# Adjacency attention on one core: scores by seven products per pair of query tiles in place of eight, with P's low halves on POOL and the mask bias on ACT

## What is computed

```
h = maximum(layernorm(x), 0)
lQ = masked_x @ Wlq ; lK = h @ Wlk ; lV = h @ Wlv + blv
local_scores = where(adj, lQ @ lK.T / 16, -1e9)        # 4096 x 4096
global_scores = gQ @ gK.T / 16 ; es = masked_x @ Wes    # two side columns
max_score = maximum(max(local_scores), global_scores, es)
le, ge, ee = exp(each - max_score) ; denom = sum(le) + ge + ee
res = le/denom @ lV + ge/denom * gV + ee/denom * (masked_x @ Wev + bev)
out = x + maximum(res, masked_x)
```

## Time and profile before

| | |
|---|---|
| median of 3 runs | 790.59 us (790.18 to 790.66) |
| span of the profiled execution | 787.8 us; the runs' median lies 2.8 us above it |
| PE busy | 760.5 us (97%) |
| DVE / ACT / POOL busy | 613.9 / 386.6 / 222.5 us (78 / 49 / 28%) |
| 16 DMA engines busy, hardware queue | 74.5% |
| granted PE clock, mean | 0.996 |

### The profile page before, as it was taken

How to read it: one execution, slowest core, us unless ns; L and a number is a source line. 1 busy time by engine, 2 the same in 40 slices (tenths; PEclk the granted TensorE clock), 3 DMA queues, 4 the chain that set the end, 5 groups by cost and what they waited for, 6 DMA issues and landing times.

```text
span 787.8 us, 15535 instructions
## 1 busy us (share of the span) xinstructions
PE 760.5 (97%) x4200; PEld 424.8 (54%) x4200; DVE 613.9 (78%) x1811; ACT 386.6 (49%) x871; POOL 222.5 (28%) x175
## 2 busy tenths in 40 slices
PE   4799999999999999999999999999999999999995
PEld 3476555555555555555555555555555555555553
DVE  5967677788777778887777788877777888777775
ACT  5757553345555444455554434555544445555442
POOL 2642222332222323322223233223232332132200
PEclk9999999999999999999999999999999999999999
DMA  9983787967778778767677786766777876778656
GB/s 268 227 155 83 145 156 145 174 140 146 144 149 160 148 152 169 147 143 148 141 164 146 154 166 140 156 137 146 162 146 158 167 148 143 143 143 168 119 119 125
DMA packets 334786, 119.92 MB, mean 152 GB/s; under 512 B 303920, under 2 KB 330672, under 8 KB 334768
## 3 DMA queue, kind: packets, MB, share of 16 engines
q1 hardware_dynamic: 334768, 119.70, 74.5%
HBM read 39.98 MB, written 4.19 MB: 56 GB/s over the span
## 4 chain that ended last, share of the span: by engine, by line
PE 82%; issue 7%; DVE 5%; DMA 4%; SPq 1%; ACT 1%; POOL 0%; DVEq 0%; POOLq 0%
PE ps_scores L555 37%; PE ps_u L573 24%; PE ps_u L575 12%; PE ps_q L531 3%; PE ps_v L589 3%; DMA shared<-shared 3%; PE ps_v L602 3%; DMA shared<-x 1%; DVE st L713 1%; DVE shared L805 1%; DVE s L780 1%; DVE w_sq L888 0%; ACT shared L437 0%; DVE q_hl L752 0%; SPq L266 0%
## 5 line engine op out<-in xcount | busy, mean ns | idle before, releaser
L555 PE MATMUL ps_scores<-hT,qT 128*128 128x512 f16 x1536 | 374.3, 380 | 4.9 <-DVE bmax L780 3.5
L573 PE MATMUL ps_u<-v_rows,shared 128*128 128x512 f16 x1024 | 346.2, 379 | 5.8 <-DMA shared<-shared 5.8
L387 POOL TENSOR_SCALAR bias<-adj,big 128x1024 f32<-128x1024 uint8 x128 | 169.8, 1327 | 495.9 <-DVE bmax L780 270.4
L575 PE MATMUL ps_u<-v_rows,shared 128*128 128x256 f16 x1024 | 279.1, 273 | 0.0
L780 DVE CUSTOM_DVE_ANT_0 s<-ps_scores,bias 128x512 f32<-128x512 f32 x256 | 176.3, 689 | 98.4 <-PE ps_scores L555 82.6
L555 PEld LDWEIGHTS ps_scores<-hT,qT 128*128 128x128 f16 x1536 | 149.8, 98 | 160.2 <-issue 6.5
L805 DVE SCALAR_TENSOR_TENSOR shared<-s,shared 128x512 f16<-128x512 f32 x256 | 192.0, 760 | 20.1 <-ACT shared L464 20.1
L454 ACT ACTIVATE s<-s,negm,invc_x 128x512 f32<-128x512 f32 x256 | 204.5, 799 | 0.0
L506 ACT ACTIVATE mass<-gs_es,negm 128x2 f32<-128x2 f32 x32 | 9.5, 296 | 362.0 <-DVE negm L799 362.0
L573 PEld LDWEIGHTS ps_u<-v_rows,shared 128*128 128x128 f16 x1024 | 100.1, 98 | 131.4 <-DMA shared<-shared 9.7
L464 ACT ACTIVATE shared<-s 128x512 f16<-128x512 f32 x256 | 154.1, 614 | 0.0
(11 more groups left out here) (75 smaller groups left out, 371.4 us busy)
## 6 DMA issues: line engine op xcount, KB each, us to landing
adj<-adj SPq DMA_DIRECT2D x32, 512.0 KB, 4.3
shared<-x SPq DMA_DIRECT2D x8, 512.0 KB, 6.1
mxT_q<-mxT SPq DMA_DIRECT2D x32, 128.0 KB, 2.6
mxT_f<-mxT SPq DMA_DIRECT2D x32, 128.0 KB, 2.2
xm<-x SPq DMA_DIRECT2D x32, 128.0 KB, 2.8
xm<-mx SPq DMA_DIRECT2D x32, 128.0 KB, 2.3
out<-o_sb SPq DMA_DIRECT2D x32, 128.0 KB, 2.3
shared<-shared SPq DMA_TRANSPOSE x128, 4.3
```

The source lines that it names most:

```text
L387: nc.gpsimd.tensor_scalar(bias[:, b * MW:(b + 1) * MW], adj8[:, k.par, b * MW:(b + 1) * MW], big[:, k.par, 0:1], big[:, k.par, 1:2], ALU.m ...
L555: last = nc.tensor.matmul(ps_scores[:, b % 2], qT[:, k.par, q_half * DC + c], hT[:, b * CPB:(b + 1) * CPB, h_half * DC + c, :], start=firs ...
L573: nc.tensor.matmul(ps_u[:, k.par], pT[:, u, 0, at + j], v_rows[:, kc, :], start=kc == 0, stop=False)
L575: last = nc.tensor.matmul(ps_u[:, k.par, 0:D], pT[:, u, 1, at + j], v_rows[:, kc, 0:D], start=False, stop=kc == NB * CPB - 1)
```

## The change

Two neighbouring query tiles are now taken together (a pair), against groups of 1024 keys. A period p is one pair and one group; there are 16 pairs of 4 groups, 64 periods. In a period the 256 x 256 by 256 x 1024 product of queries and keys (rows, channels and keys each split in two halves) has eight half products in the plain form. From period 12 on it is made by seven, by a Strassen scheme: `p1` to `p7`, each 3 matmuls of 512 columns, 21 in place of 24. Periods 0 to 11 keep the plain form (`classic`) while POOL builds sums of key halves (`keys_t1` to `keys_t4`). Partial results are read out of PSUM and added to the bias buffer on DVE (`add11`, `add12`, `add22`, 512 columns each), and four reads with maximum (`out11`, `out12`, `out21`, `out22`) finish the four quarters.

The program is unrolled. In period p the exponentials and halves of P of period p-5 are made (`LAG_E`), and P times V of period p-6 (`LAG_V`), now three matmuls of 256 columns per chunk. The low half of P (`p_low`) is made by POOL from period 12 on, 1024 columns at a time; the mask bias by ACT, 1024 columns at a time, in a ring of three buffers (`NBI`) of one tile's 1024 keys. The sum of the side terms (`rest`, ten instructions) and two additions (`add_rest`, `finish`) are on POOL, `combine` and `row_top` on DVE. The queries' seven sums and halves are split over DVE (`q_rows`), ACT (`q_scale`, `q_high`) and POOL (`q_sums`, `q_low`).

Four kinds of period follow each other from period 12 on: p mod 4 = 0 (row maximum), 1 (`project`, `q_rows`, `q_sums`), 2 (`es_values`, `combine`, `rest`, `row_top`) and 3.

```diff
+    PC = 12
+    LAG_E = 5
+    LAG_V = 6
+    NS = 5
+    NPT = 3
+    NBI = 3
...
+            def transpose_p(u):
+                sp.wait_ge(s_plo, u + 1)
+                if u >= NPT:
+                    sp.wait_ge(s_pv, u - NPT + 1)
+                sp.dma_start_transpose(pT[:, u % NPT].rearrange("p a c q -> p (a c) q"),
+                                       p_hl[:, u % 2].rearrange("p a k -> p (a k)")).then_inc(s_pT[u % NPT], 16)
...
+            def q_sums(n):
+                pool.wait_ge(s_qf, 2 * n + 2)
+                m = n - PC // NG
+                nc.gpsimd.tensor_tensor(f32q[:, S1], f32q[:, A21], f32q[:, A22], ALU.add).then_inc(s_qs, 1)
+                nc.gpsimd.tensor_tensor(f32q[:, S3], f32q[:, A11], f32q[:, A21], ALU.subtract).then_inc(s_qs, 1)
+                pool.wait_ge(s_qs, 4 * m + 1)
+                nc.gpsimd.tensor_tensor(f32q[:, S2], f32q[:, S1], f32q[:, A11], ALU.subtract).then_inc(s_qs, 1)
+                pool.wait_ge(s_qs, 4 * m + 3)
+                nc.gpsimd.tensor_tensor(f32q[:, S4], f32q[:, A12], f32q[:, S2], ALU.subtract).then_inc(s_qs, 1)
...
+            def p_low(u):
+                p = u // 2
+                pool.wait_ge(s_phi, u + 1)
+                if u and low_on_dve(u - 1):
+                    pool.wait_ge(s_plo, u)
+                nc.gpsimd.tensor_tensor(p_hl[:, u % 2, 1], s32[:, p % NS, u % 2], p_hl[:, u % 2, 0], ALU.subtract
+                                        ).then_inc(s_plo, 1)
...
+            def rest(n):
+                pool.wait_ge(s_w, n + 1)
...
+                for t in range(2):
+                    if t:
+                        pool.wait_ge(s_r, k + 5)
+                    nc.gpsimd.tensor_scalar(r12[:, t], blv_b[:, :], w3[:, t, 0:1], None, ALU.mult).then_inc(s_r, 1)
+                    nc.gpsimd.tensor_scalar(rb[:, :], gv_b[:, :], w3[:, t, 1:2], None, ALU.mult).then_inc(s_r, 1)
+                    pool.wait_ge(s_r, k + 5 * t + 2)
+                    nc.gpsimd.tensor_tensor(r12[:, t], r12[:, t], rb[:, :], ALU.add).then_inc(s_r, 1)
+                    pool.wait_ge(s_r, k + 5 * t + 3)
+                    nc.gpsimd.tensor_scalar(rb[:, :], bev_b[:, :], w3[:, t, 2:3], None, ALU.mult).then_inc(s_r, 1)
+                    pool.wait_ge(s_r, k + 5 * t + 4)
+                    nc.gpsimd.tensor_tensor(r12[:, t], r12[:, t], rb[:, :], ALU.add).then_inc(s_r, 1)
...
+            def add_rest(n):
+                pool.wait_ge(s_c2, 2 * n + 2)
+                pool.wait_ge(s_r, 10 * n + 10)
+                pool.wait_ge(s_xm, 32 * (n + 1))
+                nc.gpsimd.tensor_tensor(t_sb[:, :, :], t_sb[:, :, :], r12[:, :, :], ALU.add).then_inc(s_f, 1)
+
+            def finish(n):
+                pool.wait_ge(s_top, n + 1)
+                nc.gpsimd.tensor_tensor(t_sb[:, :, :], t_sb[:, :, :], xm[:, 0], ALU.add).then_inc(s_fin, 1)
...
+            for p in range(4, NPER + LAG_V + 1):
+                u = 2 * (p - LAG_E)
+                if 0 <= u < 2 * NPER and not low_on_dve(u):
+                    p_low(u)
+                n = (p + 3) // NG
+                if p % NG == 1 and 2 <= n < NP:
+                    if NG * n >= PC:
+                        q_sums(n)
+                    q_low(n)
+                if 0 <= u < 2 * NPER and not low_on_dve(u + 1):
+                    p_low(u + 1)
+                n = (p - 10) // NG
+                if p % NG == 2 and 0 <= n < NP:
+                    rest(n)
+                    add_rest(n)
+                    finish(n)
...
+            def mask_bias(u):
+                p, t = u // 2, u % 2
+                n = p // NG
+                if t == 0:
+                    act.wait_ge(s_adj[p % 2], ring(p, 2))
+                    act.wait_ge(s_big, 2 * n + 2)
+                if u >= NBI:
+                    v = u - NBI
+                    if v % 2 == 0:
+                        act.wait_ge(s_o11, v // 2 + 1)
+                        act.wait_ge(s_o12, v // 2 + 1)
+                    else:
+                        act.wait_ge(s_o21, v // 2 + 1)
+                        act.wait_ge(s_o22, v // 2 + 1)
+                nc.scalar.activation(bias[:, u % NBI].rearrange("p b k -> p (b k)"), adj8[:, p % 2, t], ACT.Identity,
+                                     bias=big[:, n % 2, 1, t:t + 1], scale=big[:, n % 2, 0, t:t + 1]
+                                     ).then_inc(s_bias, 1)
...
+            for p in range(4, NPER + LAG_V + 1):
+                if p < NPER:
+                    mask_bias(2 * p + 1)
+                u = 2 * (p - LAG_E)
+                live = 0 <= u < 2 * NPER
+                if live:
+                    if u % (2 * NG) == 0:
+                        act.wait_ge(s_negm, p // NG)
+                    exp_unit(u)
+                    if u % (2 * NG) == 0:
+                        side_exp((p - LAG_E) // NG)
+                    p_high(u)
+                n = (p + 3) // NG
+                if p % NG == 1 and 2 <= n < NP:
+                    q_scale(n)
+                if live:
+                    exp_unit(u + 1)
+                if p % NG == 1 and 2 <= n < NP:
+                    q_high(n)
+                for k in V_AT.get(NB + p - 3, ()):
+                    v_high(k)
+                if p + 1 < NPER:
+                    mask_bias(2 * p + 2)
+                if live:
+                    p_high(u + 1)
...
+            def product(bank, n, g, f, keys, start, stop):
+                nc.tensor.matmul(bank, q_form(n, f, 1), keys(0), start=start, stop=False, skip_group_check=True)
+                nc.tensor.matmul(bank, q_form(n, f, 0), keys(1), start=False, stop=False, skip_group_check=True)
+                return nc.tensor.matmul(bank, q_form(n, f, 0), keys(0), start=False, stop=stop, skip_group_check=True)
...
+            def p4(p):
+                n, g = p // NG, p % NG
+                pe.wait_ge(s_o22, p + 1)
+                if n == PC // NG:
+                    pe.wait_ge(s_t4, g + 1)
+                product(ps_x[:, p % 2], n, g, A22, lambda hl: mixed(g, 2, hl), False, True).then_inc(s_p4, 1)
+
+            def p5(p):
+                n, g = p // NG, p % NG
+                pe.wait_ge(s_o12, p)
+                if n == PC // NG:
+                    pe.wait_ge(s_t1, g + 1)
+                product(ps_v[:, :], n, g, S1, lambda hl: mixed(g, 0, hl), True, False).then_inc(s_p5, 1)
...
+                old = p - 1
+                if p < NPER:
+                    p1(p)
+                p_times_v(v, 0, 2)
+                if wino(old):
+                    p7(old)
+                p_times_v(v, 2, 4)
+                if p < NPER:
+                    p5(p)
+                p_times_v(v, 4, 7)
+                if p < NPER:
+                    p6(p)
+                p_times_v(v, 7, 9)
+                if wino(old):
+                    p4(old)
+                p_times_v(v, 9, 11)
+                if p < NPER:
+                    p2(p)
+                p_times_v(v, 11, 14)
+                if p < NPER:
+                    p3(p)
+                p_times_v(v, 14, 16)
...
+            def add11(p):
+                dve.wait_ge(s_p1, p - PC + 1)
+                dve.wait_ge(s_bias, 2 * p + 1)
+                at = bias[:, (2 * p) % NBI, 0]
+                nc.vector.tensor_tensor(at, ps_x[:, p % 2], at, ALU.add).then_inc(s_a11, 1)
...
+            def row_top(n):
+                dve.wait_ge(s_f, n + 1)
+                nc.vector.tensor_tensor(t_sb[:, :, :], t_sb[:, :, :], xm[:, 1], ALU.max).then_inc(s_top, 1)
...
+                    if wino(old):
+                        out12(old)
+                    if p < NPER:
+                        add11(p)
+                    if wino(old):
+                        out22(old)
+                    if p < NPER:
+                        add22(p)
+                        add12(p)
+                    if wino(old):
+                        out21(old)
+                    if p % NG == 0 and n < NP:
+                        row_max(n)
+                    m = (p + 3) // NG
+                    if p % NG == 1 and 2 <= m < NP:
+                        q_rows(m)
+                    if p < NPER:
+                        out11(p)
+                if p % NG == 1 and 0 <= (p - 9) // NG < NP:
+                    weights((p - 9) // NG)
+                if p % NG == 2 and 0 <= (p - 10) // NG < NP:
+                    row_top((p - 10) // NG)
```

1227 lines of the change are left out of this document (665 added, 562 removed).

## The result

The changed kernel takes 1088.55 us (median of four, 1083.83 to 1094.26), the kernel before on the same chip 790.38 (789.09 to 790.66): a ratio of 1.3785 [1.3737, 1.3833]. The forecast was 985, with 860 to 1045 as its range, so the sign was right and the size was not: the profiled execution (the run of 1094.26) has a span of 1092.4 us, and the sum had 988. The four runs of this kernel lie up to 10 us apart, so an experiment built on it has to move it by more than that to say something.

A forecast was written before the change was run, and what follows sets the result against it. PE's work bounded the kernel before; loops of waits between engines would bound the changed one. Period 12 near 162 us, thirteen pairs of 59.2 to 926, tail to 988, 990 with the span-median difference, stated as 985; range 860 to 1045.

The forecast's parts named there:

- The lags don't cover the change: Plain periods: the chain from `p4` to chunk 8 of the next period takes 10.7 us, so a period takes about 11.07.
- The pair, 59.2 us: Steady loop of four periods: 58.1 us of waits plus about 1 for half clock, against 45.0 before.
- `out12` in C to D's first chunk: From `out12` in p mod 4 = 3 to the first P times V chunk in p mod 4 = 0: 10.1 us.
- to chunk 8 in B: From `p4` in p mod 4 = 1 to chunk 8 in p mod 4 = 2: 15.9 us.
- to `p5` in C: From `p4` in p mod 4 = 2, through `rest`, `add_rest`, `row_top`, to `p5` in p mod 4 = 3: 15.3 us.
- The start, "period 12 starts near 162": Prologue and periods to 11: 88 us at period 4's end, later plain periods at 10.4 each, period 12 near 162.
- Thirteen pairs and the tail: From period 12: 13 x 59.2 with small corrections, 764 us, to 926; then the tail to 988 of span.
- A's stall: In p mod 4 = 1 the queries' splitting delays bias and high half; PE waits 4.8 us at the next period's chunk 8.
- PE-bound: Rival for the whole kernel: the lags hide everything and 33.7 us are won, 757; chance 0.05.
- no change: Rival for the whole kernel: each chain 1 to 3 us shorter at once, 780 to 830; chance 0.04.
- "Rest off the path": Rival for the pair: `add_rest` is through before DVE reaches `row_top`, pair 50.1 us, whole 870; chance 0.13.
- POOL slower: Rival for POOL: one-input instructions 1.2 us, two-input ones 1.15, adding 6 us a pair, 1065; chance 0.08.

The follow-up runs named there:

- The shortened rest: Changed kernel with the `bev` term of `rest` left out, one one-input and one two-input POOL instruction fewer per tile: 1035.2 us.
- constant weights: Changed kernel with the three weights per tile in POOL's six one-input `rest` instructions replaced by the constant 0.3: 1081.8 us.
- The lag of one group: Changed kernel with ACT and DVE converting V's products of a group of rows one group later in the prologue: 1074.9 us.
- the two edits together: Changed kernel with V's conversions one group later and ACT's second high half ahead of the second mask bias: 1008.3 us.
- loosened, with eight products and the low halves on DVE: Changed kernel with V conversions later, high half before bias, `rest`, `add_rest` on DVE, `q_rows` earlier, `q_high`, `q_low` later, eight products, P's low halves on DVE: 828.6 us.
- `q_rows` early: Changed kernel with only `q_rows` moved ahead on DVE by some six instructions, right behind `add11` in p mod 4 = 1: 1040.9 us.
- the side work on DVE: Changed kernel with `rest` and `add_rest` moved from POOL to DVE, and `combine`, `add_rest`, `row_top` placed behind `out22`: 946.4 us.
- the best kernel in pairs: Changed kernel with eight plain products, the order of work around them loosened, and all low halves of P on DVE: 828.6 us.

## Why the prediction missed

**The lags don't cover the change.** Right: the chain of `out21`, bias, high half, low half and transpose binds. The run with the high half before the bias shows it in the plain periods and in the pairs, which both get shorter.

**The pair, 59.2 us.** The mechanism and its places were right; 61.6 was measured, +2.4. The forecast's loop can be followed step by step in one pair. It begins with `p5` of C at 456.38, goes by these rows, by `p4` of B at 499.14 and ends with `p5` of the next C at 517.72, both shown above:

```profile
456.38 0.61 PE L683 MATMUL ps_v<-hW,qT 128*128 128x512 f16 x1 [9.49 <-DVE bmax L987]
...
466.54 0.28 PE L775 MATMUL ps_u<-v_rows,pT_base 128*128 128x256 f16 x1 [0.71 <-DMA pT_base<-p_base]
...
483.10 0.38 PE L683 MATMUL ps_x<-hW,qT 128*128 128x512 f16 x1
```

| step | forecast | measured |
|---|---|---|
| `out12` in C to D's first chunk | 10.1 | 10.2 |
| to `p4` in A | 16.4 | 16.6 |
| to chunk 8 in B | 15.9 | 15.4 |
| to `p4` in B | 0.3 | 0.6 |
| to `p5` in C | 15.3 | 18.6 |

So it was no luck that the pair came near: four of five steps agree within 0.5 us. The fifth holds `rest`, 9.2 us (505.91 to 515.07) where the sum had 6.3, and some of the 1 us that the forecast added apart for the half clock. The mis-sized term is a one-input instruction of 256 on POOL: 0.49 taken, 0.30 to 1.20 as bounds, 0.92 measured; 6 x 0.43 = 2.6 a pair. The shortened rest shows that it counts in full. The two-input ones took 0.72, as chosen. I had drawn the 0.49 from a line through two-input instructions; with constant weights the form still costs 0.85. The upper bound's 55 us would have held the truth for the pairs. The bias on ACT, taken at 1.14, held ACT for 1.13 (last section).

**The start, "period 12 starts near 162": this step failed.** PE's first matmuls of period 5 (its `project`) and of period 12:

```profile
128.92 1.98 PE L662 MATMUL ps_q<-mge,mxT_q 128*128 128x258 f32 x8 [1.62 <-DVE v_rows L1088]
...
216.89 0.47 PE L683 MATMUL ps_x<-hT,qT 128*128 128x512 f16 x1 [3.99 <-DVE bmax L987]
```

Period 12 is 55 us late, over half of the miss of 104. Of these, 41 were lost by the end of period 4 (128.9, forecast 88) and 14 in periods 5 to 11 (88.0, forecast 74). Two pieces. First, I charged the prologue 11.7 us for nine more blocks and 2 for "fuller ACT and DVE", as if PE bound it. It is a ring: PE's products of V, ACT's conversion of them in the same group of rows, then the rows of the next group on ACT, its statistics and outputs on DVE, and only then PE again:

```profile
57.67 0.60 ACT L512 ACTIVATE v_rows<-ps_q 128x512 f16<-128x512 f32 x1 [5.31 <-PE ps_q L813]
...
59.47 2.06 ACT L503 ACTIVATE p_base<-s,nb_h,rs_h 128x256 f32<-128x256 f32 x4
```

```profile
50.64 0.59 PE L683 MATMUL ps_v<-hT,qT 128*128 128x512 f16 x1 [5.34 <-DVE bmax L987]
64.66 0.58 PE L683 MATMUL ps_w<-hT,qT 128*128 128x512 f16 x1 [5.34 <-DVE bmax L987]
```

A group takes 14.0 us with 5.3 of idling, and PE works behind that idling at a lower clock: 0.50 is granted from 51 to 54 us, and a 512 takes 0.59 to 0.63 us where the earlier trace rows has 0.38. The lag of one group removed 16 us of it. Second, I took periods 6 to 11 at PE's pace of 10.4 us, although the loop that I had closed for plain periods, `out21` to bias to high half, stands in them too; first to third maxima, periods 4 to 11, took 110.9 us, 13.9 each. High half before bias took 12.5 off. Of the 55 us, the two edits together gave 34 back (third maxima 193.3 against 227.4); by itself the run with eight products, which takes the key sums off POOL, has them 22 earlier (205.7). The remaining 21 us were not taken apart; loosened, with eight products and the low halves on DVE, the third maxima come at 184.9, 42 us earlier.

**Thirteen pairs and the tail.** From period 12 to PE's first chunk behind period 63 (1022.41) the 13 pairs took 805.5 us against 764. By the pair's 61.6, 31 of these 41 are explained; where the forecast took 5 us off for the first and last pair, the trace has 5 more. The tail took 70.0 where the sum had 62; its named terms (39 for ten units, 8, 2, 3.1, 2.3) add up to 54.4 only, so 8 of its 62 us have no source. 55 + 41 + 8 are the miss.

**A's stall.** Place and size were right: PE's 4.1 against 4.8, and `q_rows` early gave back 3.7 a pair. It was that run's expectation which allowed too little for it.

**The rivals.** PE-bound (757) and no change are out. "Rest off the path" (870) was tried: 946.4 with the side work on DVE, pairs of 51.3 where I had 50.1; most of the rest of the gap is the start again (third maxima at 228.2). POOL slower (1065) had the right cause but 6 us a pair for it, where 2.4 were measured (the two-input instructions kept their 0.72), and it still lay under the truth, since it leant on the same start.

**What it would show.** PE at 75% (80% said); PE's waits for DVE ahead of `p5` 9.0 us in 15 places (8 in 14); `row_top` 11.8 each in 16 places (9 or more); `p_low` 2.13; four periods 61.6 (58 to 60). PE's waits for transposes are 43, not 12, of 2.2 us in the mean. The rule that POOL and DVE collide when DVE has two SBUF inputs (the Trainium skill, GPSIMD Engine Reference, Specifications) held: alone the two-input instructions of `rest` took 0.72, as I took them, and the one at 197.82 in the last section took 1.75.

## What to carry to other kernels

Lay out the loops of waits for the prologue and for the transition as you do for the steady part: a stretch priced at one engine's pace, while its chain crosses four engines, is where a sum goes wrong by tens of us. An algorithm with fewer products returns its outputs later and needs all of them; count the idle engines' queues between "output" and "next operand" before counting the matmuls saved. And where two units of work are joined, price the fill and the drain: here the best kernel in pairs had the steady pace of the one before and lost 38 us in its start and end, more than the 34 that seven products could have saved.
